# Loading and splitting the weights of four experts in the last pair of attention heads, in an array that shares its place with the attention's inputs

## What is computed

```python
x = x + attention(_layernorm(x), ctx, ctx, length)   # x: 2048 rows of 256, ctx: 1601 rows
x = x + experts(_layernorm(x))
```

## Time and profile before

| | us |
|---|---|
| median of three timed runs | 1307.51 |
| the profiled execution | 1304.17 |
| its span, first to last instruction | 1302.4 |
| attention: last output store issued at | 953.28 |
| projection stage: first instruction, last logits | 959.3, 1058.8 |

### The profile page before, as it was taken

One profiled execution on the slowest core, in us unless ns is written; L12 is line 12 of the kernel. 1 busy time (PEld: TensorE's weight loads), 2 busy tenths in 40 slices (PEclk: granted clock), 3 DMA queues, 4 the chain that ended last, 5 costly groups with the idle time before them and its releaser, 6 DMA issues. The chain is left out here.

```text
span 1302.4 us, 32525 instructions
## 1 busy us (share of the span) xinstructions
PE 1093.0 (84%) x12966; PEld 714.9 (55%) x12966; DVE 994.1 (76%) x1722; ACT 642.5 (49%) x1196; POOL 677.3 (52%) x474
## 2 busy tenths in 40 slices
PE   1546989989989998998998999899968742999994
PEld 0332556556656655655665665666647631666662
DVE  5736999899899899999989989999836750444441
ACT  3523655655555565555565565555645520333331
POOL 0053783684485477368458547644437637333333
PEclk9867999999999999999999999999978965999997
DMA  7034221521412422142141241221058703333331
GB/s 260 9 68 112 47 53 35 129 56 26 126 38 60 109 52 63 41 112 54 40 116 40 55 119 44 59 57 30 15 211 283 277 21 126 62 55 55 53 54 17
DMA packets 92029, 105.51 MB, mean 81 GB/s; under 512 B 45469, under 2 KB 73054, under 8 KB 91614
## 3 DMA queue, kind: packets, MB, share of 16 engines
q1 hardware_dynamic: 77166, 76.38, 22.9%
q10 hardware_dynamic: 7552, 18.51, 4.3%
q0 software_dynamic: 7152, 8.43, 3.8%
HBM read 39.46 MB, written 25.37 MB: 50 GB/s over the span
## 5 line engine op out<-in xcount | busy, mean ns | idle before, releaser
L803 DVE TENSOR_REDUCE part_max<-mx 128x1 f32<-128x427 f32 x768 | 420.2, 592 | 56.1 <-PE mx L583 55.0
L708 ACT ACTIVATE prob<-sc 128x512 f32<-128x512 f32 x640 | 347.5, 595 | 186.9 <-PE sc L571 183.1
L903 POOL TENSOR_TENSOR prob_lo<-prob 128x1024 bf16<-128x1024 f32 x128 | 249.1, 1946 | 254.1 <-ACT prob L708 254.1
L612 PE MATMUL pv<-VV,prob_lo 128*128 128x65 bf16 x2560 | 269.8, 196 | 0.0
L610 PE MATMUL pv<-VV,prob 128*128 128x65 bf16 x2560 | 268.5, 193 | 0.8 <-POOL prob_lo L903 0.6
L611 PE MATMUL pv<-VV,prob 128*128 128x64 bf16 x2560 | 268.6, 193 | 0.0
L815 DVE TENSOR_TENSOR prob_lo<-prob 128x1024 bf16<-128x1024 f32 x192 | 261.0, 1359 | 6.3 <-ACT prob L708 6.3
L583 PE MATMUL mx<-K,Q 128*128 128x427 bf16 x768 | 238.6, 350 | 27.9 <-DVE part_max L803 17.4
L610 PEld LDWEIGHTS pv<-VV,prob 128*128 128x128 bf16 x2560 | 240.6, 99 | 31.6 <-POOL prob_lo L903 0.7
L611 PEld LDWEIGHTS pv<-VV,prob 128*128 128x128 bf16 x2560 | 237.9, 97 | 27.2
L570 PE MATMUL sc<-Q,K 128*128 128x512 bf16 x640 | 244.1, 381 | 0.7 <-ACT prob L708 0.7
(11 more groups left out here) (183 smaller groups left out, 1832.1 us busy)
## 6 DMA issues: line engine op xcount, KB each, us to landing
we<-in_w_exp ACTq DMA_DIRECT2D x16, 768.0 KB, 6.3
q32s<-q SPq DMA_DIRECT2D x128, 64.0 KB, 2.0
Q<-next_q_hi SPq DMA_DIRECT2D x32, 256.0 KB, 3.7
attention_out<-o_out SPq DMA_DIRECT2D x64, 128.0 KB, 2.0
o_in<-attention_out SPq DMA_DIRECT2D x16, 512.0 KB, 5.6
expert_inputs<-zeros SPq DMA_DIRECT2D x7, 774.0 KB, 5.8
VV<-next_v SPq DMA_DIRECT2D x16, 322.5 KB, 3.8
q32s<-q SPq DMA_DIRECT2D x128, 40.0 KB, 1.9
```

The lines of the kernel that those rows point to most:

```text
L612: ins = pe.matmul(out, prob_lo[:, s % PRING, j, qt * P:(qt + 1) * P], VV[a][:, t, HD:VW], start=False, stop=t == pl.kt - 1, skip_group_che ...
L708: act.activation(prob[:, s % PRING, j, :], sc[n % 2][:], ACT.Exp, scale=HD ** -0.5).then_inc(exp_done, 1)
L803: dve.tensor_reduce(part_max[:, b_ % 2, qt, h:h + 1], mx[:, pl.part_banks(qt, h)[0]:pl.part_banks(qt, h)[-1] + 1, 0:pl.width], mybir.AxisL ...
L903: pool.tensor_tensor(prob_lo[:, s % PRING, 0:g, :], prob[:, s % PRING, 0:g, :], hi_half(prob[:, s % PRING, 0:g, :])[:, :, 1::2], ALU.subtr ...
```

## The change

One array `we` of 98304 bytes per partition takes the place of `we_hi` and `we_lo`, and is allocated for the whole kernel. The attention's inputs (XH, XL, CHI, CLO, the rotary tables, `w32`, `w_hi`, `w_lo`, `wo32`, the `next_` arrays) become views of the same bytes. The first four experts lie over XH, XL, CHI, CLO and the rotary tables. In the last pair, in each of the 8 blocks i, ACT converts half i at m = 2, POOL subtracts it at m = 3, and SP loads it into `q32` or `q32s`, which the last pair doesn't use. In the projection stage the loop over halves goes over the other 8 only, in steps 0 to 7.

```diff
+HALF = WC // 2
+EARLY = E
...
+        we = sb("we", [P, E * 2 * WC], BF16)
+        we_hi, we_lo = (we[:].rearrange("p (e h c) -> p e h c", e=E, h=2)[:, :, h, :] for h in range(2))
+        early = expert_space(we)
...
+        we32 = [buf[:].rearrange("p u c -> p (u c)")[:, 0:HALF] for buf in (q32, q32s)]
...
@@ attend, scalar
+                def expert_high(pl, n):
+                    if n == 0:
+                        act.wait_ge(pj_ready, PAIRS * pl.units)
+                        act.wait_ge(turn_done, PAIRS * QK_UNITS)
+                    act.wait_ge(we_loaded[n % 2], 16 * (n // 2 + 1))
+                    act.activation(half(we_hi, n), we32[n % 2], ACT.Copy).then_inc(we_hi_made, 1)
...
                         if m == 1 and s > pl.groups:
                             copy_out(p, i - 1)
+                        if last and m == 2 and i < EARLY:
+                            expert_high(pl, i)
@@ attend, gpsimd
+                def expert_low(n):
+                    pool.wait_ge(we_hi_made, n + 1)
+                    pool.tensor_tensor(half(we_lo, n), we32[n % 2], half(we_hi, n), ALU.subtract).then_inc(we_lo_made, 1)
...
                         if m == 1 and s > pl.groups:
                             output(p, i - 1)
+                        if last and m == pl.pool_groups[1] and i < EARLY:
+                            expert_low(i)
@@ attend, sync
+                def load_half(n):
+                    if n == 0:
+                        for u in range(4):
+                            sp.wait_ge(swapped[u], 64 * 2 * PAIRS)
+                        sp.wait_ge(sin_done, PAIRS * QK_UNITS)
+                    if n >= 2:
+                        sp.wait_ge(we_lo_made, n - 1)
+                    sp.dma_start(we32[n % 2], w_exp[n // 2, :, (n % 2) * HALF:(n % 2 + 1) * HALF]).then_inc(we_loaded[n % 2], 16)
...
                                 store(p, s // pl.groups - 1)
+                            if last and s == LAG:
+                                load_half(0)
+                                load_half(1)
+                            if last and s % pl.groups == 0 and 0 < s // pl.groups < EARLY - 1:
+                                load_half(s // pl.groups + 1)
@@ project_out, scalar
                 def load_half(n):
-                    act.dma_start(we32[:, n % WS, :], w_exp[n // 2, :, (n % 2) * HALF:(n % 2 + 1) * HALF]).then_inc(we_loaded[n % WS], 16)
+                    w = EARLY + n
+                    act.dma_start(we32[:, n % WS, :], w_exp[w // 2, :, (w % 2) * HALF:(w % 2 + 1) * HALF]).then_inc(we_loaded[n % WS], 16)
...
-                    if n < 2 * E:
+                    if n < 2 * E - EARLY:
                         act.wait_ge(we_loaded[n % WS], 16 * (n // WS + 1))
-                        act.activation(half(we_hi, n), we32[:, n % WS, :], ACT.Copy).then_inc(we_hi_made, 1)
-                        if n + 2 < 2 * E:
+                        act.activation(half(we_hi, EARLY + n), we32[:, n % WS, :], ACT.Copy).then_inc(we_hi_made, 1)
+                        if n + 2 < 2 * E - EARLY:
@@ project_out, gpsimd
-                    if n < 2 * E:
+                    if n < 2 * E - EARLY:
                         pool.wait_ge(we_hi_made, n + 1)
-                        pool.tensor_tensor(half(we_lo, n), we32[:, n % WS, :], half(we_hi, n), ALU.subtract).then_inc(we_lo_made, 1)
+                        pool.tensor_tensor(half(we_lo, EARLY + n), we32[:, n % WS, :], half(we_hi, EARLY + n), ALU.subtract).then_inc(we_lo_made, 1)
```

More of the change, by code:

```diff
@@ L153, in hi_half, with expert_space, half @@
     return ap.bitcast(BF16)
+def expert_space(we):
+    views, at = {}, 0
+    for name, d, n, dt in (("XH", DT, S, BF16), ("XL", DT, S, BF16), ("CHI", DT, LP, BF16), ("CLO", DT, LP, BF16),
+                           ("ropeq", 2, S, F32), ("ropek", 2, LP, F32), ("invalid", 1, LP, BF16),
+                           ("next_q_hi", 1, S, BF16), ("next_k_hi", 1, LP, BF16),
+                           ("next_q_lo", 1, S, BF16), ("next_k_lo", 1, LP, BF16),
+                           ("w32", 3 * DT, P, F32), ("w_hi", 3 * DT, P, BF16), ("w_lo", 3 * DT, P, BF16),
+                           ("wo32", H * HD // P, D, F32)):
+        size = d * n * (2 if dt == F32 else 1)
+        ap = we[:, at:at + size]
+        if dt == F32:
+            ap = ap.bitcast(F32)
+        views[name] = ap.rearrange("p (d n) -> p d n", d=d) if d > 1 else ap
+        at += size
+    assert at <= E * 2 * WC
+    return views
+def half(w, n):
+    return w[:, n // 2, (n % 2) * HALF:(n % 2 + 1) * HALF]
 def build(nc, x, ctx_in, length, g, b, w_pairs, b_pairs, bv_cols, wo, bo, gate, w_exp, rope, keypos, consts, out):
@@ L185, in build @@
             sb, _ = maker(upto_attend)
[L186 to L192, removed]
+            XH, XL, CHI, CLO, ropeq, ropek, invalid = (early[k] for k in ("XH", "XL", "CHI", "CLO", "ropeq", "ropek", "invalid"))
             validc = sb("validc", [P, KT])
-            w32 = sb("w32", [P, 3, DT, P])
-            w_hi = sb("w_hi", [P, 3, DT, P], BF16)
-            w_lo = sb("w_lo", [P, 3, DT, P], BF16)
+            w32, w_hi, w_lo = (early[k].rearrange("p (k d) n -> p k d n", d=DT) for k in ("w32", "w_hi", "w_lo"))
             bqk = sb("bqk", [P, 2])
-            wo32 = sb("wo32", [P, H * HD // P, D])
+            wo32 = early["wo32"]
             w_loaded, w_hi_made, w_lo_made = sem("w_loaded"), sem("w_hi_made"), sem("w_lo_made")
@@ L467, in attend @@
     x_slots, zeros, zeroed = (have[k] for k in ("x_slots", "zeros", "zeroed"))
+    w_exp, we_hi, we_lo, early = (have[k] for k in ("w_exp", "we_hi", "we_lo", "early"))
     with ExitStack() as ctx:
@@ L475, in attend @@
         VV = [sb(f"VV_{a}", [P, KT, VW], BF16) for a in range(2)]
-        next_hi = [sb("next_q_hi", [P, S], BF16), sb("next_k_hi", [P, LP], BF16)]
-        next_lo = [sb("next_q_lo", [P, S], BF16), sb("next_k_lo", [P, LP], BF16)]
+        next_hi = [early["next_q_hi"], early["next_k_hi"]]
+        next_lo = [early["next_q_lo"], early["next_k_lo"]]
         next_v = sb("next_v", [P, 2, KT, VW], BF16)
@@ L523, in attend @@
         o_stored = [sem("o_stored0"), sem("o_stored1")]
+        we_loaded = [sem("early_we_loaded0"), sem("early_we_loaded1")]
+        we_hi_made, we_lo_made = sem("early_we_hi_made"), sem("early_we_lo_made")
+        we32 = [buf[:].rearrange("p u c -> p (u c)")[:, 0:HALF] for buf in (q32, q32s)]
         def set_of(block_):
@@ L1040, in experts @@
         "x", "gate", "w_exp", "o_dram", "out", "wo_hi", "wo_lo", "bob"))
-    ident, ident_b, eps_col, rank8, cst, x_slots, zeroed = (have[k] for k in (
-        "ident", "ident_b", "eps_col", "rank8", "cst", "x_slots", "zeroed"))
+    ident, ident_b, eps_col, rank8, cst, x_slots, zeroed, we_hi, we_lo = (have[k] for k in (
+        "ident", "ident_b", "eps_col", "rank8", "cst", "x_slots", "zeroed", "we_hi", "we_lo"))
     with ExitStack() as both:
@@ L1060, in project_out @@
     w_exp, we_hi, we_lo = (have[k] for k in ("w_exp", "we_hi", "we_lo"))
-    HALF = WC // 2
     wo_hi, wo_lo, bob = (have[k] for k in ("wo_hi", "wo_lo", "bob"))
@@ L1093, in project_out @@
         we_hi_made, we_lo_made = sem("we_hi_made"), sem("we_lo_made")
-        def half(w, n):
-            return w[:, n // 2, (n % 2) * HALF:(n % 2 + 1) * HALF]
         STEPS = ST + 5
```

2 lines of the change are left out of this document (removed).

## The result

| | before | after |
|---|---|---|
| median of four runs, us | 1307.84 | 1342.47 |
| lowest and highest | 1307.23, 1308.71 | 1335.52, 1345.72 |
| the profiled execution | 1304.17 | 1344.14 |

The change makes the kernel slower: the ratio after to before is 1.026, 95% interval 1.0238 to 1.0282. That is +34.6 us, where +25.0 was forecast.

The account below looks back on a forecast made before the run. A tight chain through DVE and PE bounds the last pair's blocks, with ACT and POOL half free; 13.5 + 4.0 + 18.5 + 3.5 - 14.5 = +25.0 us gave 1332.5 us, range +7.5 (1315) to +38.5 (1346).

Parts of the forecast that it names:

- stall (Part 2): Start of the last pair: ACT waits for the load of half 0, so line 720 comes 13.5 us late (12.4 to 16.3).
- low clock behind the stall, and block 0: First block of the last pair: half-speed PE after the stall, and collision with POOL's subtraction, together 4.0 us (2.5 to 6).
- blocks 1 to 5 (Part 3): Last pair: POOL's split holds DVE's line 815, ACT's conversion adds 0.25; 3.7 us a block, 18.5 us in all.
- blocks 6 and 7: End of the last pair: splits still hold a line 815, the last stands before POOL's last output; 3.5 us (1 to 6).
- relief of the projection stage (Part 1): Projection stage: eight halves leave, shortening steps 8 to 15 by 9.3 us and the tail by 5.2; 14.5 us saved.
- a rival with 2.5 us a block: Last pair's blocks: PE's idle stretches bring a clock fall in most blocks, total +37.5, 1345 us; chance 0.17.
- The signs of being wrong: ACT's first expert conversion before 882, blocks 1 to 5 under 12 us, or projection stage saving over 17 us.
- The first rival: Last pair: splits fall into gaps of DVE, leaving ACT's 0.7 us a block; +6.5, 1314 us; chance 0.14.
- The other side: Projection stage relief of 17 us exceeds a 12.4 us stall, no line 815 held; -4.6, 1303 us; chance 0.05.

Follow-up runs that it names:

- the run with the fill: Useless PE products added in blocks 1 to 5, against the changed kernel with the first loads issued earlier; 1324.47 us, ratio 1.014 to the kernel before.
- half subtraction: Changed kernel with early loads, POOL subtracting only 768 of 1536 columns of each half, other low halves zeroed; 1301.92 us, ratio 0.9977 to the kernel before.
- other place: Changed kernel with early loads, POOL's whole subtraction moved behind its `prob_lo` of slot 1 of the next block; 1304.49 us, ratio 1.0003 to the kernel before.

## Why the prediction was right, and where it was off

The sign, the order of the terms and the range held. Slower was given 0.92, and 1342.47 lies in 1315 to 1346, but 10 us over the forecast. By its own steps, where the attention's +50.4 is 13.96 + 3.01 + 29.4 + 4.1:

| step of the prediction | expected | measured in after |
|---|---|---|
| stall (Part 2) | 13.5 | 13.96 |
| low clock behind the stall, and block 0 | 4.0 | 3.0 |
| blocks 1 to 5 (Part 3) | 18.5 | 29.4 |
| blocks 6 and 7 | 3.5 | 4.1 |
| relief of the projection stage (Part 1) | -14.5 | -15.9 |

**The stall** was right in part by luck, as its errors cancel. The load took 6.8 us, not 5.3, so above the middle of the earlier trace rows. SP came to it 0.9 us sooner than I put it, of which 0.5 is only that this trace stood 0.50 us ahead; measured from the row before, the stall is 14.46 us and not 13.5. In the second trace in which the same load stands behind the seven others (no subtraction, loads as in the change) it lands after 6.9 us; issued in the pair before, after 6.0. The 4.2 us that I had worked out from the Trainium skill's page "DMA: Bandwidth & Descriptors" (Where 436 GB/s comes from; Latency and other measured facts) was further off. The loads into `q` in after, of which the first is the slow one, by the view of that tile:

```profile
DMA to landing us min/median/max: 4.2/4.8/6.7
```

Only the fastest of the four shows 4.2.

**Block 0** came out at 3.0 us and I had put 4.0, of which 3.4 for the clock. The run without the subtraction has these 3.0 whole, so no collision is in them, and the 1.0 us by which a line 849 is held in block 0 of after (2.25 us) is hidden; with the conversion's 0.5 taken off, some 2.5 us are the clock's.

**The term that was mis-sized is the block of Part 3,** 3.7 us where 5.9 came. Its holds were right to 0.02 us a block in sum (3.60 expected, 3.58 measured), singly less so (2.52 and 1.08 expected, 2.31 and 1.27 measured). ACT's conversion costs 0.5 and not 0.25: I reasoned that PE's later max row would cover a part of its 0.72, and it covers less. And the forecast had no clock in these blocks. I had that as a rival with 2.5 us a block and gave it 0.17, since "the idle is in pieces, of which only one would reach 1.8 us". Both were true, 0.93 and 1.84 us, and it was enough: the clock falls in each block, and the run with the fill puts its price at 2.2 us. So that rival was the case that came, with its size and its sum of 1345 close to the measurement; it should have had more weight than the forecast. The evidence stood in the front rows: 1.57 us of idle ahead of 8 us at 0.57. I had read that as something of the projection stage, and not as a price for one such piece in a busy stretch. Yet PE is busy there without a gap from 980 to 991, at clock 1.00, before the 1.57 us.

The signs of being wrong could not have caught this: none of the three came true, though the term was off by 10.9 us. Two small slips stand in the prediction besides. The first rival's terms add up to +6.4 and not +6.5, so its 1314 lies just under the range that is said to reach down to it. And DVE has all three subtractions between 898.52 and 906, not two (the third at 904.79); that no gap between them holds 3.10 us is right.

**The relief** came out 1.4 us larger, with its two parts off in opposite directions. From step 8 to step 15 it is 27.2 us instead of 38.7, so -11.6 where I had -9.3: after the last split the first two steps take only 3.3 us each, as the stage catches up, and then 4.11, in which PE is busy without a gap as the earlier trace rows had it. The tail gave 3.9, not 5.2. The wait of 3.66 us is gone, but the clock is 0.80 there (0.71 before), with PE busy 9.73 of 12.12 us. The other 0.5 lies ahead of step 8. But 1.4 us is less than this stage varies by: in the seven kernels above with the same code in it and nothing zeroed it takes 89.8 to 94.0 us, so the relief is 11.7 to 15.9 from trace to trace, and the 14.5 was not shown to be wrong.

**The rivals.** The first, that the splits fall into gaps, was wrong for the change as made, and right for the same work cut in three and placed: with the holds and the stall gone the kernel is at 0.9953. The other side, a relief larger than what the attention loses, is seen there too: without stall and holds only the conversions' 0.5 us a block and a dearer end, 3.3 us, stand against a relief of 15.3 us in that trace.

What stays open: what decides, besides PE's idle pieces, whether the clock falls, and why the mixture's time varies by up to 9.5 us and the projection stage's by 4 with the same code. The last makes small gains of these kernels hard to tell apart.

## What to carry to other kernels

Before work goes onto a half-idle POOL, look at what it reads and at what DVE does in those very microseconds: the price of a subtraction of 3.1 us was 5.6, 1.0 (half its columns), 0.7 to 1.2, or nothing in a block, by its place and its pieces, and 3 to 4.5 us once at the attention's end for a whole half in another place or in pieces. When an added hold makes PE idle, price the clock with it: idle pieces of 0.93 and 1.84 us in a block went here with a fall of the clock that cost another 2.2 us each time. And a load whose user sits in front of the critical row should be issued where its buffer comes free, not where the new stage begins; that alone was worth 13.8 us at the place where it was needed, and 10.4 us at the attention's end (both counted from the row before the stall).

## What was not expected of the hardware

- The granted clock falls to the 1.2 GHz level in the middle of a stretch in which PE is 83% busy (14.09 of 17.01 us), behind idle pieces of 0.93 and 1.84 us. With longest pieces of 0.56, 0.64 and 1.01 us (half subtraction, fill, other place) it stayed at 1.00 in the blocks. Pieces of 1.28 and 1.48 us came with a fall in one block and without one in another.
- The fall comes again in each block: 17.03 to 17.06 us in five blocks in a row of the kernel with the first loads earlier, which did not come out of it by itself. Without the fall 14.82 to 14.84 us was as steady (one block 15.03), with the same work and nine products more, and 14.83 us in the block behind them, with the same work and none.
- Clearing 3072 columns on POOL (2.66 us) does not hold a two-operand subtraction on DVE (1.23 us), while subtracting 1536 (3.11 us) does (3.53 us).
